# Two ScalarE steps of an attention stage moved later: the inverse of the denominators and the second copies of the keys

## What is computed

```python
keys    = einsum('bse,neh->bsnh', residual, W_key) + Bias_key
queries = einsum('bse,neh->bsnh', residual, W_query) + Bias_query
values  = einsum('bse,neh->bsnh', residual, W_values) + Bias_values
scores  = einsum('bknh,bqnh->bnqk', keys, queries) / sqrt(H)
scores  = where(causal_mask, EPS, scores)      # q_idx < k_idx: EPS, not -inf
probs   = softmax(scores, axis=3)
weighted = einsum('bnqk,bknh->bqnh', probs, values)
out     = einsum('bqnh,nhe->bqe', weighted, W_output) + Bias_output
```

## Time and profile before

| | |
|---|---|
| median of 3 runs | 2258.28 us (2254.77 to 2260.71) |
| profiled execution, own time | 2256.03 us |
| its span | 2254.2 us |
| PE matmul, share of the span | 88% |
| PE weight load | 52% |
| DVE | 64% |
| ACT | 43% |
| POOL | 25% |
| chain that ended last: PE | 62% |
| chain that ended last: DVE, ACT | 15%, 6% |

### The profile page before, as it was taken

The page is one execution under the profiler, slowest core; times in us unless marked ns, Lnnn a source line. Parts: engine busy times, 40 slices in busy tenths (PEclk is TensorE's granted clock), DMA queues, the critical chain, the costliest instruction groups (busy, mean ns, idle before and its releaser), DMA issues.

```text
span 2254.2 us, 31789 instructions
## 1 busy us (share of the span) xinstructions
PE 1987.2 (88%) x10080; PEld 1177.1 (52%) x10080; DVE 1439.8 (64%) x2432; ACT 970.6 (43%) x1358; POOL 573.6 (25%) x543
## 2 busy tenths in 40 slices
PE   6899999996997999997779999999969889999975
PEld 3444444443784555556644444444438755555554
DVE  6677788866317776852377777778662377777432
ACT  2444454441224666561234444544413246656411
POOL 0000000000001787884120000000000037797831
PEclk7999999998886999997969999999979779999977
DMA  3366665678000000000514666666760000000015
GB/s 92 81 152 156 146 147 143 141 162 242 5 1 10 5 6 6 1 1 29 157 37 116 143 148 143 149 151 152 172 201 1 1 10 10 2 6 1 1 61 149
DMA packets 84846, 187.99 MB, mean 83 GB/s; under 512 B 17697, under 2 KB 46754, under 8 KB 83106
## 3 DMA queue, kind: packets, MB, share of 16 engines
q1 hardware_dynamic: 83650, 183.76, 32.5%
q0 software_dynamic: 1024, 2.10, 0.3%
HBM read 178.47 MB, written 8.91 MB: 83 GB/s over the span
## 4 chain that ended last, share of the span: by engine, by line
PE 62%; DVE 15%; issue 11%; ACT 6%; DMA 3%; SPq 1%; POOL 1%; DVEq 0%; ACTq 0%; POOLq 0%
PE PS L794 9%; PE PS L766 5%; PE PS L730 5%; PE PS L905 3%; DVE mx L1836 3%; PE PS L965 3%; PE PS L945 3%; PE PS L751 3%; PE PS L756 3%; PE PS L1136 3%; PE PS L948 2%; PE PS L1191 2%; DMA V<-weight_rows 2%; PE PS L860 2%; DVE mrow L1969 2%
## 5 line engine op out<-in xcount | busy, mean ns | idle before, releaser
L1836 DVE TENSOR_REDUCE mx<-PS 128x8 f32<-128x512 f32 x512 | 329.6, 684 | 178.3 <-PE PS L730 167.3
L2335 POOL TENSOR_TENSOR Esum<-Esum,EE 128x512 f32<-128x512 f32 (+3 forms) x320 | 337.8, 1084 | 14.7 <-POOL Esum L2335 10.1
L1865 DVE TENSOR_TENSOR EE<-EE,V 128x1024 f32<-128x1024 f32 x256 | 302.7, 1217 | 47.2 <-DMA V<-weight_rows 46.4
L1457 ACT ACTIVATE EE<-PS 128x1024 f32<-128x1024 f32 x256 | 260.1, 1024 | 143.6 <-PE PS L756 141.7
L2289 POOL TENSOR_TENSOR U<-xn,norm_aff 128x1024 f32<-128x1024 f32 x2 | 4.7, 2354 | 1073.0 <-DVE QA L2260 1073.0
L794 PE MATMUL PS<-EE,Vlater 128*64 128x512 f32 x1024 | 252.8, 612 | 9.6 <-ACT U L1423 8.3
L1969 DVE TENSOR_REDUCE mrow<-PS 128x1 f32<-128x512 f32 (+3 forms) x384 | 202.6, 550 | 84.6 <-PE PS L908 65.6
L730 PE MATMUL PS<-KA,QA 128*128 128x512 f32 x512 | 203.3, 451 | 28.2 <-DVE mx L1836 21.9
L751 PE MATMUL PS<-QA,KA 128*128 128x512 f32 x512 | 185.3, 443 | 0.0
L1541 ACT ACTIVATE EE<-PS 128x1024 f32<-128x1024 f32 (+2 forms) x192 | 137.8, 738 | 103.8 <-PE PS L948 101.6
L756 PE MATMUL PS<-QB,KB 80*128 80x512 f32 x512 | 163.6, 401 | 0.0
(11 more groups left out here) (306 smaller groups left out, 3311.9 us busy)
## 6 DMA issues: line engine op xcount, KB each, us to landing
V<-weight_rows SPq DMA_DIRECT2D x512, 256.0 KB, 5.5
EE<-in_w SPq DMA_DIRECT2D x48, 192.0 KB, 2.8
V<-in_Wg SPq DMA_DIRECT2D x4, 1024.0 KB, 6.3
EE<-in_Wu SPq DMA_DIRECT2D x4, 1024.0 KB, 11.6
EE<-in_Wd SPq DMA_DIRECT2D x4, 1024.0 KB, 13.6
sorted_out<-U SPq DMA_DIRECT2D x12, 256.0 KB, 3.2
wo<-in_wo SPq DMA_DIRECT2D x5, 512.0 KB, 3.7
wq_s<-in_wq SPq DMA_DIRECT2D x17, 128.0 KB, 2.8
```

What stands on the lines that cost most here:

```text
L1457: act.activation(EE[i % 2][:, t, :], banks(2 * (t % 2)), ACT.Exp, scale=QSCALE).then_inc(s["p2_exp"], 1)
L1836: dve.tensor_reduce(mx[:, t, half * 8:half * 8 + 8], banks(5 + x % 2, BANK).rearrange("p (c k) -> p c k", c=8), AX, ALU.max).then_inc(s["p ...
L1865: dve.tensor_tensor(EE[i % 2][:, t, :], EE[i % 2][:, t, :], weight_ring[a % 2][:, odd, :], ALU.mult).then_inc(p3_mul, 1)
L2335: ins = pool.tensor_tensor(Esum[:, h, lo:hi], Esum[:, h, lo:hi], e_tile(t)[:, h, lo - t * P:hi - t * P], ALU.add)
```

## The change

ScalarE's order within a pair of the second attention. `inverse(p - 1)` (pairs 1 to 7) stood behind the exponents of tile 2 and now stands behind those of tile 3. `second_k(p + 1)` (pairs 0 to 6) stood behind it and now stands between the exponents of tile 6 and those of tile 7. No instruction is added or taken out, and the other engines' streams and all waits stay as they are written.

```diff
                     exponents(p, 1, 1)
                     exponents(p, 2, 0)
                     exponents(p, 2, 1)
+                    exponents(p, 3, 0)
+                    exponents(p, 3, 1)
                     if prev:
                         inverse(p - 1)
-                    if follows:
-                        second_k(p + 1)
-                    exponents(p, 3, 0)
-                    exponents(p, 3, 1)
                     exponents(p, 4, 0)
                     exponents(p, 4, 1)
                     exponents(p, 5, 0)
...
                         high_q(p + 2, 0)
                     exponents(p, 6, 0)
                     exponents(p, 6, 1)
+                    if follows:
+                        second_k(p + 1)
                     exponents(p, 7, 0)
                     exponents(p, 7, 1)
                     if follows:
```

## The result

| | before | after |
|---|---|---|
| median | 2260.71 us (2254.77 to 2262.59, 5 runs) | 2269.18 us (2267.92 to 2273.97, 5 runs) |
| ratio after / before | | 1.0046, 95% interval 1.0028 to 1.0064 |
| profiled execution, own time | 2256.03 us | 2269.78 us |
| its span | 2254.2 us | 2267.9 us |

The change makes the kernel slower by 0.46% by the ratio, whose interval is 6 to 14 us; by the medians it is 8.5 us, where +5.0 was forecast, and 13.75 between the two profiled executions. So in what follows the range of the runs stands beside each median, and the second attention is read by itself in the traces.

The account below looks back on a forecast made before the run. PE's order sets the second attention's pace, so its few holes count. Terms -13.8 - 4.3 + 18.6 + 3.4 + 1.1 = +5.0 us, on a 2258.28 median: 2263.3 us, range 2257 to 2269.

Parts of the forecast that it names:

- The wait taken away: PE's scores(4, 0) no longer wait for ACT's tile 3 exponents; 1.15 us in pairs 1 to 6, both batches: -13.8 us.
- The wait behind it: PE's maxima unit 12 no longer waits for DVE, held in diagonal 3's copy, in pairs 1 to 6: -4.3 us.
- the hole of DVE stays: Rival, 12%: maxima unit 12 still waits for DVE, so the 4.3 us don't come: 2267.6 us.
- The wait put in its place: values(p, 0) wait for the later logarithm: 1.55 us twelve times, +18.6, and 1.70 twice in pair 7, +3.4 us.
- The end of the pair: At DVE's diagonal 6 copy beside POOL's product: four pairs' shift swallowed (-0.6), pair 3 +1.24 for +0.40 (+1.7): +1.1 us.
- all the copies lose their slot: Rival, 9%: in pairs 1 to 5 DVE's end-of-pair copy waits out another POOL product, 1.3 us: +10.4, 2273.7 us.
- The key copies: About 2.0 us of ACT time behind tile 6's exponents fit its wait for PE, 0.6 left: cost 0.
- The clock falls: Rival, 4%: PE's fourteen pauses of 1.5 us or more bring 1.2 GHz, 1.73 us each: +24, 2287 us.
- a clock under 1.00 between 800 and 1000: Sign of being wrong: PE's granted clock in the second attention, 1.00 (2.4 GHz) before, falls below that.

Follow-up runs that it names:

- e1: Only the key copies moved behind tile 6's exponents, inverse left behind tile 2's, against the kernel before: 2241.26 us, ratio 0.9931; run again 2243.13 us, ratio 0.9937.
- e3: The changed kernel plus 8 small matmuls (14 in pair 7), result overwritten, in the wait before values(p, 0): 2258.53 us, ratio 1.0006 to the kernel before.
- e2: Only the inverse moved behind tile 3's exponents, key copies back behind tile 2's, against the kernel before: 2292.59 us, ratio 1.0141.
- e7: e2 plus 28 filler matmuls (36 in pair 7), result overwritten, in each wait before values(p, 0): 2278.47 us, ratio 1.0086 to the kernel before.
- e9: e1 with DVE's copy of diagonal 6 moved behind the pair's last maxima and top: 2247.5 us, ratio 0.9943 to the kernel before.
- e10: e9 plus 12 filler matmuls, result overwritten, ahead of a pair's first maxima: 2231.85 us, ratio 0.99 to the kernel before.
- e6: The changed kernel with the inverse one exponent earlier, between the two heads of tile 3: 2245.61 us, ratio 0.9961 to the kernel before.

## Why the prediction was wrong

It gave 2263.3 us, no measurable change, with +6.8 us as the edge, and 0.30 for slower; the median is 2269.18. Of the 5.9 us between, 2.4 are the kernel before itself, whose median was 2258.28 in the three runs that the forecast stood on and 2260.71 in five. By its own steps:

- **The wait taken away** (-13.8): right. L945's waits for L1541 are 0.4 us in sum. What the text did not ask is which of the two moved steps makes the hole; e1 shows that it was the key copies alone.
- **The wait behind it** (-4.3): right. Unit 12 has no wait at 781.09, so the rival *the hole of DVE stays* is out.
- **The wait put in its place** (+18.6 and +3.4): right. 1.53 us in pairs 1, 3 and 5 against 1.55, with the logarithm from exponents' start + 0.60 and PE 0.09 behind its end; pair 7 waits 1.75 and costs 1.78, against 1.70. Pairs 2, 4 and 6 wait 1.66 to 1.70, a tenth more than the term, for a reason that is open.
- **The end of the pair** (+1.1): right in the pattern. Pair 3 grew from 39.52 to 40.64, +1.12 for a forecast of +1.24, and in the way told. Timelines of DVE and POOL, end of pair 3, changed kernel, against the earlier trace rows:

```profile
874.68 0.97 DVE L1994 COPY_PREDICATED EE<-consts,F 128x256 f32<-128x256 int32 x1
...
874.07 2.69 POOL L2305 TENSOR_TENSOR U<-U,xn 128x512 f32<-128x512 f32 x2
```

  The copy took 0.97 instead of 0.58 and ended at 875.65, 0.23 behind POOL's first product (874.07 + 1.35 = 875.42). The other middle pairs were 0.2 to 0.3 us longer, not 0 to 0.1. The rival that all the copies lose their slot is out.
- **The key copies** (0): right. Timeline of ACT, pair 2, changed kernel, against the earlier trace rows:

```profile
833.06 0.85 ACT L1541 ACTIVATE EE<-PS 128x256 f32<-128x256 f32 x2 [1.37 <-PE PS L948]
833.94 1.06 ACT L1522 ACTIVATE KB<-KA 64x1024 fp32r<-64x1024 f32 x1
834.90 1.04 ACT L1522 ACTIVATE KD<-KC 64x1024 fp32r<-64x1024 f32 x1
836.55 0.50 ACT L1541 ACTIVATE att_in<-PS 128x128 f32<-128x128 f32 x2 [0.60 <-PE PS L948]
```

  ACT still waits 0.60 us for PE before tile 7, to the tenth what was forecast.
- **The step that failed** is the clock: the sum put it at nothing, and the rival *The clock falls* was given 4%, dismissed with "after 0.94 no such thing is seen, and the stretch stays at 1.00", and priced as all or nothing, "at 1.73 us each" over fourteen. The size of one was near (1.6). But the trace of before had rows for pauses of 0.94 and of 4.87 us only, the new pauses lie between them, and a value between two ends was no ground for 4%. And it is no matter of all or none: five falls came, at 4 of 14 waits and once in the output matmuls, 8 us, which takes the steps' +5.8 to +14 in the profiled executions. A case "a third of the waits fall, +7" belonged in the forecast, and it would have moved chance from the same to slower. The prediction did name "a clock under 1.00 between 800 and 1000" as a sign of being wrong, and it came: 0.99 over 900 to 1000. Such a mean all but hides a fall; stretches of 4 us show it.

That the falls are the cause and not a companion is shown by e3 against the changed kernel: same order, same late values, the pauses filled, and 7 us gone from the pairs, 10 from the ratio. It holds for the four falls at the waits, not for the one in the output matmuls, which e3, too, has in one batch. With e2 and e7 the same holds for a longer pause, with e9 and e10 at another place in the pair.

## What to carry to other kernels

Before a step is moved later on one engine, list everyone who waits for it, by shared banks as well as by data; here the values waited for the logarithm, and the one half of the change that nobody waited for, the key copies, is worth some 15 us alone. A pause of TensorE has two prices, its own length and, in some of its occurrences, some 1.6 us lost to a low clock behind it; when pauses grow from under one to over one and a half us, give the partial case a real chance and look in stretches of a few us. Where a pause can't be avoided, harmless matmuls in it are cheap and worth a try.

## What was not expected of the hardware

- **Falls of the clock behind short pauses.** Behind waits of 1.5 to 1.75 us TensorE fell to 1.2 GHz for about 3.4 us in 4 of 14 cases, and partly in other ones when the same kernel ran again. Over the traces of all kernels in which `values(p, 0)` wait with nothing to fill the pause, it fell at 2 of 24 waits of 1.53 us, at 8 of 24 of 1.66 to 1.70, at 7 of 8 of 1.75 (all in pair 7) and at 10 of 12 of 2.65 to 2.79. Waits of 0.5 to 1.0 us in e6 had none, nor had the twelve of 0.94 before; but 0.8 us in e9 had five in ten, and in 11 of the 14 traces the clock also fell in output matmuls with no wait before them. So a longer pause makes a fall more likely, but its length alone doesn't decide it; what else does is open. The Trainium skill, "TensorE: Matmul & The Clock Gate", Part 1, says that the engine is throttled by default and that activity releases it; the runs with fillers agree (e3, e7 and e10 lost their falls where the matmuls were added). The falls in the output matmuls, with no wait before them, it doesn't explain.
- **A predicated copy held by a GpSimd product.** The same copy takes 0.43 us with POOL out of the way and up to 1.73 beside it, and at the end of a pair it ends 0.23 us behind the end of the product that runs (875.65 against 875.42). The Trainium skill, "SBUF — State Buffer", on the shared port pair, has a DVE operation with two SBUF inputs wait out a GpSimd one; these rows agree.
- **A wait can carry the wrong name.** Ten of the fourteen waits of L965 are put down to a copy of a diagonal by DVE, in eight that of tile 3, which the values of tile 0 don't need. It was merely the last to end before PE went on. In pair 1, where it was still running (to 778.27, PE at 777.14), the view names nobody, and the wait is as long.
